# A new setup order in a fused block (tile 0 normalised ahead of the weight splits, MLP matrices loaded later, gates and splits in pieces), and 79 expert tiles in place of 80

## The reference

```python
mod = (silu(c) @ wmod).reshape(1, 6, 1, -1)
sa, ca, ga, sb, cb, gb = (mod[:, i] for i in range(6))
ga, gb = (2 * (g >= 0) - 1) * maximum(abs(g), 0.25)     # both gates
h = layernorm(x) * (1 + ca) + sa
x = x + ga * attn(h)     # retention, 16 heads of 16, then an MLP 256 -> 1024 -> 256
h = layernorm(x) * (1 + cb) + sb
x = x + gb * ffn(h)      # 16 experts of 176, top 4 by softmax, and a shared expert of 704
```

## Time and profile before

| | us |
|---|---|
| median of 3 runs | 664.97 |
| lowest, highest | 664.3, 666.75 |
| the profiled execution, its own time | 666.45 |
| the profiled execution, its span | 664.3 |
| PE busy in the span | 550.3 (83%) |
| DVE busy | 480.5 (72%) |
| ACT busy | 285.6 (43%) |
| POOL busy | 323.4 (49%) |
| mean granted clock of TensorE | 0.92 of full |

### The profile page before, as it was taken

The page is one execution under the profiler, slowest core; times in us unless marked ns, Lnnn a source line. Parts: engine busy times, 40 slices in busy tenths (PEclk is TensorE's granted clock), DMA queues, the critical chain, the costliest instruction groups (busy, mean ns, idle before and its releaser), DMA issues.

```text
span 664.3 us, 14436 instructions
## 1 busy us (share of the span) xinstructions
PE 550.3 (83%) x4154; PEld 480.5 (72%) x4155; DVE 480.5 (72%) x1194; ACT 285.6 (43%) x696; POOL 323.4 (49%) x391
## 2 busy tenths in 40 slices
PE   2668889889898899998489979896999999999700
PEld 0357677777776788987368768685999999999600
DVE  1377978878774379898667787656677677777568
ACT  2323644454554665544135434434444444444300
POOL 1235567767665637445117777730344444444500
PEclk8788989999999999999589989996899999999955
DMA  9311212121499052111127666876644444443187
GB/s 316 135 41 41 73 50 62 58 79 39 138 315 300 2 151 74 56 49 63 56 65 224 206 187 178 252 221 224 200 130 137 119 129 131 125 124 103 71 344 296
DMA packets 66298, 92.42 MB, mean 139 GB/s; under 512 B 8528, under 2 KB 55504, under 8 KB 66256
## 3 DMA queue, kind: packets, MB, share of 16 engines
q1 hardware_dynamic: 56048, 69.86, 35.3%
q0 software_dynamic: 6912, 19.01, 7.7%
q10 hardware_dynamic: 3296, 3.03, 1.4%
HBM read 53.82 MB, written 35.95 MB: 135 GB/s over the span
## 4 chain that ended last, share of the span: by engine, by line
PE 31%; DVE 10%; issue 3%; ACT 3%; DMA 3%; SPq 0%; POOL 0%; DVEq 0%; ACTq 0%; POOLq 0%
PE bank L2025 12%; PE bank L2043 4%; PE bank L1764 4%; DVE wda_lo L1990 4%; PE bank L1780 3%; PE bank L2045 3%; PE bank L2009 3%; PE bank L2035 3%; ACT s_a_hi L1571 1%; DVE hid L1681 1%; DVE s_a_lo L1687 1%; DMA stage<-shared_d 1%; DMA stage<-expert_gu 1%; DMA wgu_hi<-results 1%; DVE sh L1697 1%
## 5 line engine op out<-in xcount | busy, mean ns | idle before, releaser
L1893 POOL DMA_INDIRECT results<-yb,xe x80 | 76.7, 959 | 111.0 <-DVE yb L1972 107.4
L1542 POOL DMA_INDIRECT dispatched<-rows,slot x64 | 67.9, 1060 | 34.6 <-issue 14.9
L2025 PE MATMUL bank<-wgu_hi,xT_hi 128*128 x160 | 60.7, 379 | 5.3 <-DVE xT_lo L1953 5.3
L1966 DVE TENSOR_TENSOR e_hT_lo<-bank,e_hT_hi 128x256 fp32r<-128x256 f32 x80 | 34.0, 425 | 33.5 <-ACT e_hT_hi L1926 33.4
L2025 PE MATMUL bank<-wgu_lo,xT_hi 128*128 x160 | 53.2, 332 | 0.0
L2025 PE MATMUL bank<-wgu_hi,xT_lo 128*128 x160 | 53.0, 332 | 0.0
L699 DVE TENSOR_TENSOR probs<-bank,causal 128x512 f32<-128x512 f32 x64 | 42.2, 684 | 10.0 <-PE bank L872 10.0
L1926 ACT CAST e_hT_hi<-bank 128x256 fp32r<-128x256 f32 x80 | 29.9, 373 | 41.2 <-PE bank L2035 41.1
L1921 ACT ACTIVATE e_sg<-bank 128x176 f32<-128x176 f32 x80 | 25.4, 318 | 51.5 <-PE bank L2025 51.5
L570 POOL TENSOR_TENSOR orms<-omse,neghalf 128x16 f32<-128x16 f32 x16 | 46.7, 2919 | 1.7 <-POOL omse L567 0.8
L1764 PE MATMUL bank<-h3T_hi,wsg_hi 128*128 128x512 f32 x88 | 36.9, 420 | 6.1 <-ACT hid L1568 2.1
(11 more groups left out here) (234 smaller groups left out, 1872.3 us busy)
## 6 DMA issues: line engine op xcount, KB each, us to landing
dispatched<-fill SPq DMA_DIRECT2D x20, 520.0 KB, 10.0
xe<-dispatched SPq DMA_DIRECT2D x80, 130.0 KB, 2.3
trig<-t_trig SPq DMA_DIRECT2D x16, 512.0 KB, 3.7
stage<-expert_gu SPq DMA_DIRECT2D x16, 352.0 KB, 3.5
wgu_hi<-results SPq DMA_DIRECT2D x11, 512.0 KB, 8.3
xt<-L_attn_x SPq DMA_DIRECT2D x32, 128.0 KB, 2.8
wgu_lo<-results SPq DMA_DIRECT2D x5, 512.0 KB, 16.6
x_rows<-h_all SPq DMA_DIRECT2D x16, 128.0 KB, 2.0
```

The costliest lines, as they stand in the source:

```text
L1542: pool.indirect_dma_start(out=dram["dispatched"], out_offset=bass.IndirectOffsetOnAxis(ap=slot[:, k, t:t + 1], axis=0), in_=rows[:, t, :], ...
L1893: pool.indirect_dma_start(out=dram["results"], out_offset=bass.IndirectOffsetOnAxis(ap=xe[r][:, E:E + 1].bitcast(INT), axis=0), in_=yb[:, ...
L1966: nc.vector.tensor_tensor(hT[1][:, q, :], hT_bank[p][:, 0:2 * P], hT[0][:, q, :].bitcast(F32), ALU.subtract).then_inc(S["h_lo"], 1)
L2025: mm = nc.tensor.matmul(gu_bank[p][:, 0:GU], xT[xn_][:, p, k, :], wgu[wn][:, k, e, :], start=(k == 0 and i == 0), stop=(k == KB - 1 and i ...
```

## The change

Five things are done. SP's first transfers are in another order, and the two MLP matrices wait for the first `h_all`. Tile 0 is normalised by DVE ahead of the splits of `wq`, and DVE waits for the tables later. The three modulation products are spread: `modulation(1)` goes ahead of body 0 on PE. The gates and the splits of `wf1` and `wf2` are cut in pieces, moved to the place in front of `rope(t)`, and spread over the bodies 0 to 7, of which eight are now written out. The expert pipeline runs over 79 tiles: its loop has three turns, and bodies 64 to 82 are written out.

```diff
+EUSED = ETILES - 1
@@ retention: pipeline and pieces
-        for t in range(6):
+        for t in range(HEAD):
...
-        with eng.Fori(3, NT // 2) as j:
+        with eng.Fori(HEAD // 2, NT // 2) as j:
+    HEAD = 8
+    HALF1, QUART2 = F // 2, FB // 4
@@ SP (ccol and rw come first in both)
+        mlp.ahead.load_spare()
+        load_x(0, 0)
         for k in range(KB):
             sp.dma_start(wq32[:, k, :], io["qkvg"][k * P:k * P + P, :]).then_inc(S[f"wq_in{k}"], 16)
-        load_x(0, 0)
         load_trig(0, 0)
+        for c in (1, 2):
+            sp.dma_start(wmod[:, :, 2 * c * E:2 * c * E + 2 * E], wmod_rows[:, :, 2 * c * E:2 * c * E + 2 * E]).then_inc(S[f"wmod_in{c}"], 16)
         load_x(1, 1)
-        sp.dma_start(fw[:, :], io["L0_attn_final_norm_w"]).then_inc(S["fw_in"], 16)
-        sp.dma_start(wmod[:, :, 2 * E:6 * E], wmod_rows[:, :, 2 * E:6 * E]).then_inc(S["wmod_in1"], 16)
         sp.dma_start(wo32[:, :, :], io["L0_attn_out_w"].rearrange("(k p) n -> p k n", p=P)).then_inc(S["wo_in"], 16)
         load_trig(1, 1)
-        mlp.ahead.load_spare()
+        sp.dma_start(fw[:, :], io["L0_attn_final_norm_w"]).then_inc(S["fw_in"], 16)
+        sp.wait_ge(S["h"], 1)
         sp.dma_start(w2_32, io["L0_attn_fc2_w"].rearrange("(k p) n -> p k n", p=P)).then_inc(S["w2_in"], 16)
         sp.dma_start(w1_32[:, :, :], io["L0_attn_fc1_w"].rearrange("(k p) n -> p k n", p=P)).then_inc(S["w1_in"], 16)
@@ ACT
-            if t == 1:
-                keep_mod(1)
                 keep_mod(2)
-            if t == 4:
-                act.wait_ge(S["w2_ga"], 1)
-                nc.scalar.copy(wf2[0][:, :, :], w2_32).then_inc(S["w2_hi"], 1)
-            if t == 3:
+            if t in (2, 3):
                 act.wait_ge(S["w1_in"], 16)
                 act.wait_ge(S["fw_in"], 16)
-                for k in range(KB):
-                    nc.scalar.activation(wf1[0][:, k, :], w1_32[:, k, :], ACT.Identity, scale=fw[:, k:k + 1]).then_inc(S["w1_hi"], 1)
+                k = t - 2
+                nc.scalar.activation(wf1[0][:, k, :], w1_32[:, k, :], ACT.Identity, scale=fw[:, k:k + 1]).then_inc(S["w1_hi"], 1)
+            if t in (4, 5):
+                for n in (2 * t - 8, 2 * t - 7):
+                    act.wait_ge(S["w2_ga"], n + 1)
+                    nc.scalar.copy(wf2[0][:, part2(n), :], w2_32[:, part2(n), :]).then_inc(S["w2_hi"], 1)
...
             if live(3): square_x2(t - 3, q)
+            if isinstance(t, int) and t == 0:
+                keep_mod(1)
             if live(0): gate(t, p)
@@ DVE (low_weights as it is with the change; gate(g, gated) is the four instructions of a gate)
+            if t == 0:
+                dve.wait_ge(S["mod_sb"], 2)
+                gate(modb[:, 2, :], modb[:, 2, :])
+            if t == 1:
+                dve.wait_ge(S["mod_sb"], 3)
+                gate(modb[:, 5, :], gb[:, :])
+                nc.vector.tensor_scalar(modb[:, 4, :], modb[:, 4, :], 1.0, None, ALU.add).then_inc(S["gates"], 1)
+            if t in (2, 3):
                 dve.wait_ge(S["w2_in"], 16)
+                dve.wait_ge(S["gates"], 3)
+                for n in (2 * t - 4, 2 * t - 3):
+                    nc.vector.tensor_tensor(w2_32[:, part2(n), :], w2_32[:, part2(n), :], modb[:, 2, :].unsqueeze(1).broadcast_to([P, QUART2, E]),
+                                            ALU.mult).then_inc(S["w2_ga"], 1)
+            if t in (4, 5):
+                for n in (2 * t - 8, 2 * t - 7):
+                    k, cols = part1(n)
                     dve.wait_ge(S["w1_hi"], k + 1)
+                    nc.vector.scalar_tensor_tensor(wf1[1][:, k, cols], w1_32[:, k, cols], fw[:, k:k + 1], wf1[0][:, k, cols].bitcast(F32),
...
+            if t in (6, 7):
+                for n in (2 * t - 12, 2 * t - 11):
+                    dve.wait_ge(S["w2_hi"], n + 1)
+                    nc.vector.tensor_tensor(wf2[1][:, part2(n), :], w2_32[:, part2(n), :], wf2[0][:, part2(n), :].bitcast(F32), ALU.subtract).then_inc(S["w2_lo"], 1)
@@ DVE body
-            if isinstance(t, int):
-                low_weights(t)
             if live(0): stats(t, p)
             if first:
-                dve.wait_ge(S["tables"], ALL_TABLES)
-                dve.wait_ge(S["prep"], PREP)
-                low_projections(0)
                 first_gain()
             if live(0): centre(t, p)
             if live(3): split_yT(t - 3, q)
             if live(0): modulate(t, p)
             if first:
+                low_projections(0)
                 low_projections(1)
+                dve.wait_ge(S["tables"], ALL_TABLES)
+                dve.wait_ge(S["prep"], PREP)
+            if isinstance(t, int) and t == 1:
+                low_out()
...
             if live(1): mask(t - 1, 2)
+            if isinstance(t, int):
+                low_weights(t)
             if live(0): rope(t, p)
@@ PE
         modulation(0)
+        pe.wait_ge(S["wmod_in1"], 16)
+        modulation(1)
...
-            if isinstance(t, int) and t == 1:
-                pe.wait_ge(S["mod_sb"], 3)
...
             if live(4): transpose_x2(t - 4, p)
+            if isinstance(t, int) and t == 1:
+                pe.wait_ge(S["mod_sb"], 3)
             if live(1): state_update(t - 1, q)
...
             if isinstance(t, int) and t == 0:
-                pe.wait_ge(S["wmod_in1"], 16)
-                modulation(1)
+                pe.wait_ge(S["wmod_in2"], 16)
                 modulation(2)
@@ experts, all engines
-        with eng.Fori(1, ETILES // XR) as j:
+        whole = EUSED // XR * XR
+        with eng.Fori(1, EUSED // XR) as j:
...
-        for t in range(ETILES, ETILES + LAG):
-            body(t, t % XR, lambda lag, t=t: t - lag < ETILES)
+        for t in range(whole, EUSED + LAG):
+            body(t, t % XR, lambda lag, t=t: t - lag < EUSED)
```

More of the change, by code:

```diff
@@ L311, in attention @@
     b_s = [bank[n] for n in (4, 5, 3, 1)]
-    names = """rwk wq_in0 wq_in1 fw_in wo_in w1_in w2_in wq_hi wq_lo wo_hi wo_lo w1_hi w1_lo w2_ga w2_hi w2_lo eps tables vecs wmod_in0 wmod_in1 x_in0 x_in1 trig_in0 trig_in1
+    names = """rwk wq_in0 wq_in1 fw_in wo_in w1_in w2_in wq_hi wq_lo wo_hi wo_lo w1_hi w1_lo w2_ga w2_hi w2_lo eps tables vecs wmod_in0 wmod_in1 wmod_in2 x_in0 x_in1 trig_in0 trig_in1
         silu_c mod_ps mod_sb sgn gates prep
@@ L628, in first_gain, with gate @@
             step("sgn", nc.vector.tensor_scalar(modb[:, 1, :], modb[:, 1, :], 1.0, None, ALU.add))
-        def gates():
-            dve.wait_ge(S["mod_sb"], 3)
-            for g, gated in ((modb[:, 2, :], modb[:, 2, :]), (modb[:, 5, :], gb[:, :])):
-                step("sgn", nc.vector.tensor_scalar(sign[:, :], g, 0.0, 2.0, ALU.is_ge, ALU.mult))
-                step("sgn", nc.vector.tensor_scalar(sign[:, :], sign[:, :], 1.0, None, ALU.subtract))
-                step("sgn", nc.vector.tensor_tensor(g, g, sign[:, :], ALU.mult))
-                step("gates", nc.vector.scalar_tensor_tensor(gated, g, 0.25, sign[:, :], ALU.max, ALU.mult))
-            nc.vector.tensor_scalar(modb[:, 4, :], modb[:, 4, :], 1.0, None, ALU.add).then_inc(S["gates"], 1)
+        def gate(g, gated):
+            step("sgn", nc.vector.tensor_scalar(sign[:, :], g, 0.0, 2.0, ALU.is_ge, ALU.mult))
+            step("sgn", nc.vector.tensor_scalar(sign[:, :], sign[:, :], 1.0, None, ALU.subtract))
+            step("sgn", nc.vector.tensor_tensor(g, g, sign[:, :], ALU.mult))
+            step("gates", nc.vector.scalar_tensor_tensor(gated, g, 0.25, sign[:, :], ALU.max, ALU.mult))
@@ L639, in low_weights, with low_out @@
+        def low_out():
+            dve.wait_ge(S["wo_hi"], 1)
+            nc.vector.tensor_tensor(wo[1][:, :, :], wo32[:, :, :], wo[0][:, :, :].bitcast(F32), ALU.subtract).then_inc(S["wo_lo"], 1)
+            dve.wait_ge(S["wo_lo"], 1)
         def low_weights(t):
+            if t == 0:
+                dve.wait_ge(S["mod_sb"], 2)
+                gate(modb[:, 2, :], modb[:, 2, :])
             if t == 1:
-                dve.wait_ge(S["wo_hi"], 1)
-                nc.vector.tensor_tensor(wo[1][:, :, :], wo32[:, :, :], wo[0][:, :, :].bitcast(F32), ALU.subtract).then_inc(S["wo_lo"], 1)
@@ L644, in low_weights @@
-                dve.wait_ge(S["wo_lo"], 1)
-            if t == 2:
-                gates()
-            if t == 3:
-                dve.wait_ge(S["w2_in"], 16)
-                dve.wait_ge(S["gates"], 1)
-                nc.vector.tensor_tensor(w2_32, w2_32, modb[:, 2, :].unsqueeze(1).broadcast_to([P, FB, E]), ALU.mult).then_inc(S["w2_ga"], 1)
-            if t == 5:
-                dve.wait_ge(S["w2_hi"], 1)
-                nc.vector.tensor_tensor(wf2[1][:, :, :], w2_32, wf2[0][:, :, :].bitcast(F32), ALU.subtract).then_inc(S["w2_lo"], 1)
@@ L655, in low_weights @@
-            if t == 4:
-                for k in range(KB):
+                dve.wait_ge(S["mod_sb"], 3)
+                gate(modb[:, 5, :], gb[:, :])
+                nc.vector.tensor_scalar(modb[:, 4, :], modb[:, 4, :], 1.0, None, ALU.add).then_inc(S["gates"], 1)
```

(12 more changed lines are left out.)

11 lines of the change are left out of this document (6 added, 5 removed).

## The result

The changed kernel takes 648.79 us, median of 4 runs (648.15 to 649.27). The kernel before took 665.66 beside it (4 runs, 664.3 to 666.75). The ratio is 0.9747, 95% interval 0.9725 to 0.9769. That is 16.9 us faster. Forecast were 654.8 us and a range of 649.5 to 660.5, so the direction was right and the gain was larger than the range allowed. The two profiled executions differ by 18.3 us (spans 664.3 and 646.0, own times 666.45 and 648.15).

A forecast was written before the change was run, and what follows sets the result against it. Setup was taken as bound by order, then the retention as a ring where any member's delay carries to the end. The terms summed to -10.1 us, from the median 664.97 to 654.8, range 649.5 to 660.5.

The forecast's parts named there:

- tile 0: Setup to first rotary product: earlier `h_all` lets ACT's square follow the tables, -4.3, and a faster projection clock, 0.3; together -4.6.
- tile 1: Body 1: scores 2.3 us earlier with one modulation product ahead, less 1.2 for second gate and addition; net -1.1.
- tile 2: Body 2: gate instructions and cold projection gone from its head, one piece added; 11.4 us for 15.22, -3.8.
- tiles 3 to 5: Whole splits at the heads replaced by a piece each; bodies of 11.8 us, 35.4 for 38.6, -3.2.
- tiles 6 and 7: Bodies 6 and 7, plain before, now carry a piece each: +2.9.
- clock: Bodies 2 to 7: PE idles longer ahead of the transposes, so two falls of its clock in six bodies, +1.7.
- experts: Expert pipeline: one tile less, -2.0; the written-out last fifteen counted as nothing, bounds -0.9 to +0.5.
- I give this body the plain 10.37: Body 2's base: the last body without setup work, 10.37 us, less 0.4 for missing output work, plus 1.4 for a piece.
- Rival (b): Tile 0: tables land early, near 12 us, and first projection runs at upper clock; 2 to 3.5 us more, about 651; 0.14.
- (c): Bodies 2 to 7: clock falls in nearly all (3.6 us) or ACT's pieces delay `kT` (2 us); 659; chance 0.18.
- (d): Slower than before: PE runs all of bodies 2 to 7 at 1.2 GHz, 18 us in all; 671; chance 0.04.
- (e): Experts: written-out code costs, fifteen tiles at 2.2 us in place of 2.0; 658; chance 0.04.

The follow-up runs named there:

- whole splits: Changed kernel with the MLP splits whole again at the head of bodies 3, 4 and 5, six bodies written out: 655.36 us, ratio 0.9772.
- the changed kernel's second: The changed kernel, nothing altered, run again as the measure for other runs on the same chip: 648.53 us, ratio 0.9734 to the kernel before.
- the 24 small instructions: Changed kernel with all sixteen bodies written out, low halves and gating as 24 instructions of 128x256, two in each of bodies 3 to 14: 637.86 us, ratio 0.9579.
- the run of its own: Kernel before with 79 expert tiles alone, the last fifteen and the pipeline's tail written out: 663.36 us, ratio 0.9963.

## Why the prediction was right in direction and too small

The table compares its terms with the profiled pair, in us.

| step | predicted | measured |
|---|---|---|
| tile 0 | -4.6 | -5.45 |
| tile 1 | -1.1 | -1.6 |
| tile 2 | -3.8 | -4.4 |
| tiles 3 to 5 | -3.2 | -5.5 |
| tiles 6 and 7 | +2.9 | +1.35 |
| clock | +1.7 | 0 |
| experts | -2.0 | -3.1 |
| sum | -10.1 | -18.7 |

The measured steps sum to 0.4 more than the 18.3 of the spans; 0.3 of it is lost between the retention and the experts. Between the medians the gain is 16.9: the profiled execution of the kernel before was slower than its median and that of the changed kernel faster.

**The step that failed: "I give this body the plain 10.37"**, and by it 11.8 for each of bodies 3 to 7. The plain body was read from a loop, and the bodies that carry pieces are written out. A written-out plain body takes 9.90, as the runs with 14 and 16 bodies written out show. Over bodies 2 to 7 this is 2.8 us. It also hid a part of the change that the prediction priced at nothing: two more bodies leave the loop, which is 0.9 of the 2.8. The mechanism "a piece costs its time less DVE's idle time" was right. Its size was a little off: in bodies 4 to 7 it is 1.48 to 1.55 from start to start less 0.31, that is 1.15 to 1.2 for the 1.43 that was taken; bodies 2 and 3 took 0.95 and 0.98 more than 9.90. The 0.4 that the prediction took off body 2 for missing output work is not there: without a piece, written out, this body takes 9.85 or 9.86. All six pieces cost 6.7 us where 8.6 less that 0.4 were counted, 1.5 less. Together, 4.3 us, they are the misfit of bodies 2 to 7 (8.5 gained where 4.1 net were forecast), and they turn 11.8 into 11.1.

**The clock, +1.7, did not come.** The prediction took the fall in body 5 of the kernel before, behind a stretch with PE busy 1.91 us of 4, for a sign of what pieces would do. There PE had stood idle for 2.06 us; with pieces it stands idle for 1.5 us in body 2 and for 1.0 to 1.2 in bodies 3 to 7, and the clock stayed. That falls are real the run with doubled pieces shows, and also the one with whole splits, whose body 5 took 12.94 us after 12.34 for body 4 (first pair of rows). But one fall in one trace does not say that the next execution has it. The kernel before with its last expert tiles written out has the same retention code as the kernel before, and PE busy 1.95 of the same 4 us, but no fall (second pair):

```profile
70.00:74.00 4.00, 2.26 (x21) 1.78 (x16) 3.83 (x5) 2.41 (x7) 1.04 (x3) 1.00 0.34 131
74.00:78.00 4.00, 3.40 (x42) 3.17 (x43) 3.32 (x10) 1.32 (x5) 2.64 (x5) 0.66 0.14 37
```

```profile
82.00:86.00 4.00, 1.95 (x39) 1.59 (x37) 3.59 (x10) 1.76 (x7) 0.88 (x3) 1.00 0.28 90
86.00:90.00 4.00, 3.52 (x23) 2.96 (x22) 3.69 (x9) 1.38 (x5) 3.77 (x5) 1.00 0.03 9
```

Its body 5 took 12.22 us where the kernel before took 13.25, so a fall costs about 1.0 us, for the 0.9 of the prediction. The price was right, the number of falls was mis-sized: none for two, 0 us for 1.7.

**Tile 0.** The tables (14.0 foreseen, 14.30 seen), `h_all` (11.8, 10.82) and the hidden splits and gate came as said. The clock term was 0.3; in the profiled execution it was 1.2, in others nothing. Rival (b) was half right: the projection warm (at 2.4 GHz), the tables not early. That the profiled execution was a warm one is chance, as far as these runs show. Warm or cold decides 2.2 us: the rotary product of tile 1 begins at 30.3 to 31.3 in the six warm executions and at 32.6 to 33.3 in the three cold ones (the changed kernel's second, the whole splits, the 24 small instructions).

**Tile 1.** The scores begin 4.71 us after the first rotary product (24.49 after 19.78), before it was 7.41: -2.7 for the -2.3 of the prediction. The net is -1.6 for -1.1, so 1.1 were given back, for the 1.2 foreseen; the second gate and the addition take 1.77 us of DVE (28.81 to 30.58), where it had idled 0.57.

**Experts**: the tile is right by the run of its own (2.5 measured, its written-out tiles included, interval 1.5 to 3.4, for 2.0). The written-out tiles gave about 1, at the edge of the bound of -0.9 and within the scatter of two executions. Rivals (c), (d) and (e) are out: in the changed kernel no body of 12 us, no low clock in bodies 2 to 7, no price of fetching.

## What to carry to other kernels

A base for "plain plus added work" has to be read from code of the same form: a looped body and a written-out one differ here by 5%, and a change that moves the border between them has that as a term of its own. Wait last for what comes last, above all in a loop, where a satisfied wait behind the late one can still cost a queue entry of about 0.1 us. Side work belongs into an engine's own waits, in instructions about as long as these (0.41 to 0.48 us in waits of 0.35), rather than in one place in front of the ring's next member; in this kernel that was worth six more microseconds for the same work. And a fall of the clock seen in one trace is not yet a property of the kernel: the same retention code showed the clock's fall in body 5 in one execution and not in another.
